# One row-tiled block per two heads in the first attention stage, with PSUM banks that change roles each cycle

## The reference

```
q = norm(x) @ Wq;  k, v = split(ctx @ Wkv)          # 16 heads of 64
p = softmax(q_h k_h^T / 8) over 12544 keys
x = x + concat_h(p v_h) @ Wo + bo
```

## Time and profile before

| what | value |
|---|---|
| median of 3 runs | 1464.38 us |
| the profiled execution's own time | 1462.08 us |
| its span, first to last instruction | 1460.4 us |
| TensorE busy | 1402.6 us, 96% |
| VectorE busy | 1067.2 us, 73% |
| ScalarE busy | 835.6 us, 57% |
| GpSimd busy | 599.9 us, 41% |
| granted TensorE clock, mean | 0.991 |

### The profile page before, as it was taken

One profiled execution on the slowest core, in us unless ns is written; L12 is line 12 of the kernel. 1 busy time (PEld: TensorE's weight loads), 2 busy tenths in 40 slices (PEclk: granted clock), 3 DMA queues, 4 the chain that ended last, 5 costly groups with the idle time before them and its releaser, 6 DMA issues. The chain is left out here.

```text
span 1460.4 us, 28153 instructions
## 1 busy us (share of the span) xinstructions
PE 1402.6 (96%) x11057; PEld 1200.8 (82%) x11057; DVE 1067.2 (73%) x2050; ACT 835.6 (57%) x1594; POOL 599.9 (41%) x521
## 2 busy tenths in 40 slices
PE   8999999999999999999999999999998889999778
PEld 7888888888888888888888888888886779999558
DVE  5777777777777777777777777777785656677774
ACT  4666666666666666666666666666662236666411
POOL 4353433435353434353535343443420427765220
PEclk9999999999999999999999999999999999999889
DMA  5000000000000000000000000000013502111720
GB/s 195 2 12 15 1 26 1 27 1 26 1 27 1 27 1 26 2 26 2 26 2 26 1 3 25 2 26 1 2 55 126 232 7 89 58 61 36 331 94 5
DMA packets 11256, 59.39 MB, mean 41 GB/s; under 512 B 2346, under 2 KB 4723, under 8 KB 10100
## 3 DMA queue, kind: packets, MB, share of 16 engines
q1 hardware_dynamic: 11124, 57.59, 10.7%
HBM read 57.45 MB, written 0.13 MB: 39 GB/s over the span
## 5 line engine op out<-in xcount | busy, mean ns | idle before, releaser
L344 POOL CAST V<-Vraw 128x512 fp32r<-128x512 f32 x189 | 115.7, 612 | 591.0 <-ACT Vraw L435 491.5
L525 DVE TENSOR_TENSOR pT<-ps,pT 128x896 fp32r<-128x896 f32 x224 | 244.4, 1091 | 140.2 <-ACT pT L427 140.0
L427 ACT ACTIVATE pT<-ps 128x896 fp32r<-128x896 f32 x224 | 205.6, 918 | 121.8 <-PE ps L606 121.0
L435 ACT COPY Vraw<-ps 128x512 f32<-128x512 f32 x189 | 111.0, 587 | 264.3 <-PE ps L586 264.3
L345 POOL TENSOR_TENSOR V<-Vraw,V 128x512 fp32r<-128x512 f32 x189 | 241.9, 1280 | 15.1
L470 DVE TENSOR_REDUCE nmx<-ps 128x1 f32<-128x896 f32 x224 | 241.9, 1080 | 0.0
L404 ACT ACTIVATE prob<-ps,nm 128x896 f32<-128x896 f32 x224 | 224.2, 1001 | 0.0
L621 PEld LDWEIGHTS ps<-pT,V 128*128 128x128 f32 x1568 | 214.9, 188 | 9.3 <-ACT d_kT L411 1.1
L621 PE MATMUL ps<-pT,V 128*128 128x256 f32 x1568 | 219.9, 279 | 0.7 <-ACT d_kT L411 0.7
L478 DVE TENSOR_REDUCE xn<-ps 128x128 f32<-128x256 f32 x224 | 95.0, 424 | 103.1 <-PE ps L621 103.1
L677 PE MATMUL ps<-ident,prob 64*128 64x64 f32 x3136 | 145.2, 229 | 4.1 <-ACT prob L404 2.6
(11 more groups left out here) (325 smaller groups left out, 2446.3 us busy)
## 6 DMA issues: line engine op xcount, KB each, us to landing
raw<-in_ctxT SPq DMA_DIRECT2D x16, 896.0 KB, 4.6
d_raw<-in_ctxT SPq DMA_DIRECT2D x12, 896.0 KB, 4.6
w<-in_w SPq DMA_DIRECT2D x2, 4096.0 KB, 19.4
wg<-in_wg SPq DMA_DIRECT2D x1, 4352.0 KB, 18.3
wu<-in_wu SPq DMA_DIRECT2D x1, 4352.0 KB, 28.1
wd<-in_wd SPq DMA_DIRECT2D x1, 4352.0 KB, 37.9
e_ea<-in_alog SPq DMA_DIRECT2D x1, 2048.0 KB, 7.2
d_mrow<-in_mask SPq DMA_DIRECT2D x14, 112.0 KB, 4.5
```

What stands on the lines that cost most here:

```text
L344: link(pool, nc.gpsimd.tensor_copy(v_high(g, i), by_head(Vraw[:, j % 2, :])), "pool_chain")
L427: nc.scalar.activation(by_row(pT[u % 2][:, :, 0, :]), pT_ps, ACT.Copy).then_inc(sem("pTh_ready"), 1)
L525: nc.vector.tensor_tensor(by_row(pT[u % 2][:, :, 1, :]), pT_ps, by_row(pT[u % 2][:, :, 0, :]).bitcast(F32), ALU.subtract).then_inc(sem("pT ...
```

## The change: what it does

Two heads, e = 2c and o = 2c + 1, now make one cycle. TensorE's order in a cycle is: transposes of e, scores of the next pair, transposes of o with four turned-back sums, and then, all with 128 rows, values, piece, weighted sum of e, values, piece, weighted sum of o. The products with 64 rows stand in one block per two heads.

Both heads' probabilities must exist at once, so there are two `prob` buffers. The banks 4 to 7 change roles from cycle to cycle: the turned probabilities of e lie in one pair of banks (4 and 5, or 6 and 7), those of o in the other; values, pieces and weighted sums go into the same banks once the turned probabilities in them are copied and split. The turned-back sums move to the tails of the score banks 0 to 3. Pieces run five steps ahead. A weighted sum now runs in its own cycle. To make space for the second `prob`, `raw` holds `aq`, `ak`, `av` and `disti` once the last context chunk is split: three loads of 256 KB and two small index patterns move from the start to the end of the stage, and SyncE waits for the loads.

The diff, cut to its core:

```diff
-    AHEAD = 4
+    AHEAD = 5
+    cycles = steps // 2
-        prob = sb("prob", [P, 2, HK], F32, keep)
+        prob = [sb(f"prob{i}", [P, 2, HK], F32, keep) for i in range(2)]
-        pT_ps = ps[:, 4:6, 0:HK].rearrange("p s (t q) -> p s t q", q=P // 2)
-        O_ps = ps[:, 4:6, HK:512]
-        OT_ps = ps[:, 6, 0:2 * P]
+        def banks(c):
+            return (4, 5) if c % 2 == 0 else (6, 7)
+        def turned_banks(u):
+            return banks(u // 2 + u % 2)
+        def value_bank(u):
+            return banks(u // 2)[0]
+        def sum_of(u):
+            bank = 5 if u == steps - 1 else banks(u // 2 + 1 - u % 2)[0]
+            return ps[:, bank, 0:2 * P]
+        def back_of(u):
+            odd = 1 if u >= steps - 2 else u % 2
+            return ps[:, 0:4, HK:512].rearrange("p (s a) n -> p a s n", a=2)[:, odd, :, :]
         def piece_bank(p):
-            return 4 + p % 4 if p < AHEAD else 7
+            return 4 + p % 4 if p < AHEAD else banks((p - AHEAD) // 2)[1]
...
# SyncE, behind the loop over chunks
+                sp.wait_ge(sem("cT_split"), 2 * (chunks + 2))
+                for name in ("aq", "ak", "av"):
+                    sp.dma_start(v[name], t[name]).then_inc(sem("band_in"), 16)
+                sp.wait_ge(sem("band_in"), 96)
...
# ScalarE
+                exp_step(1)
+                for c in range(cycles):
+                    e, o = 2 * c, 2 * c + 1
+                    act.wait_ge(sem("p_turned"), e + 1)
+                    nc.scalar.activation(by_row(pT[0][:, :, 0, :]), turned(e), ACT.Copy).then_inc(sem("pTh_ready"), 1)
+                    act.wait_ge(sem("p_turned"), o + 1)
+                    nc.scalar.activation(by_row(pT[1][:, :, 0, :]), turned(o), ACT.Copy).then_inc(sem("pTh_ready"), 1)
+                    if e in v_steps:
+                        copy_values(e)
...
+                    if e + AHEAD < steps:
+                        high_parts(e + AHEAD)
+                    if e + 2 < steps:
+                        exp_step(e + 2)
+                    if o in v_steps:
+                        copy_values(o)
...
+                    if o + 2 < steps:
+                        exp_step(o + 2)
+                    if o + AHEAD < steps:
+                        high_parts(o + AHEAD)
# VectorE
+                for c in range(cycles):
+                    e, o = 2 * c, 2 * c + 1
+                    if c >= 1:
+                        add_parts(o - 2)
+                        if o - 2 + AHEAD < steps:
+                            low_parts(o - 2 + AHEAD)
+                    dve.wait_ge(sem("pTh_ready"), e + 1)
+                    nc.vector.tensor_tensor(by_row(pT[0][:, :, 1, :]), turned(e),
+                                            by_row(pT[0][:, :, 0, :]).bitcast(F32), ALU.subtract).then_inc(sem("pTl_ready"), 1)
+                    add_denominator(e)
+                    if c >= 1:
+                        update_sums(e - 2)
+                        update_sums(o - 2)
+                    dve.wait_ge(sem("pTh_ready"), o + 1)
+                    nc.vector.tensor_tensor(by_row(pT[1][:, :, 1, :]), turned(o),
+                                            by_row(pT[1][:, :, 0, :]).bitcast(F32), ALU.subtract).then_inc(sem("pTl_ready"), 1)
+                    if e + 2 < steps:
+                        max_step(e + 2)
+                    if e + AHEAD < steps:
+                        low_parts(e + AHEAD)
+                    if o + 2 < steps:
+                        max_step(o + 2)
+                    add_denominator(o)
+                    add_parts(e)
...
# TensorE; turn(u) is the 14 transposes, for odd u with turn_sums(u - 3) and turn_sums(u - 2)
+                for c in range(cycles):
+                    e, o = 2 * c, 2 * c + 1
+                    pe.wait_ge(sem("exp_done"), e + 1)
+                    if c >= 1:
+                        pe.wait_ge(sem("o_added"), e - 1)
+                    turn(e)
+                    pe.wait_ge(sem("exp_done"), o + 1)
+                    if c + 1 < cycles:
+                        scores(c + 1)
...
+                    elif o - 2 + AHEAD < steps:
+                        pe.wait_ge(sem("kl_ready"), o - 2 + AHEAD + 1)
...
+                    turn(o)
+                    if e in v_steps:
+                        pe.wait_ge(sem("pTl_ready"), e + 1)
+                        next_values(e)
...
+                    if e + AHEAD < steps:
+                        pe.wait_ge(sem("pTl_ready"), e + 1)
+                        next_piece(e + AHEAD)
+                    pe.wait_ge(sem("pTl_ready"), o + 1)
+                    weighted_sum(e)
+                    if o in v_steps:
+                        if e in v_steps:
+                            pe.wait_ge(sem("vraw_ready"), v_steps.index(e) + 1)
+                        next_values(o)
...
+                    if o + AHEAD < steps:
+                        pe.wait_ge(sem("kl_ready"), o + AHEAD)
+                        next_piece(o + AHEAD)
+                    if o in v_steps:
+                        pe.wait_ge(sem("vraw_ready"), v_steps.index(o) + 1)
...
+                    weighted_sum(o)
```

More of the change, by code:

```diff
@@ L423, in _ @@
                         exp_step(0)
[L425 to L444, removed]
@@ L519, in _, with add_denominator @@
                 max_step(1)
-                for u in range(steps):
+                def add_denominator(u):
                     h, b = u % H0, u % 8
[L522 to L532, removed]
                     if u >= H0:
@@ L657, in _ @@
                 scores(0)
+                piece(4)
                 pe.wait_ge(sem("wv_left"), 2)
@@ L667, in _, with turn @@
                 pe.wait_ge(sem("wv_right"), 1)
[L668 to L674, removed]
+                def turn(u):
                     for k in range(NT):
-                        for s, rows in enumerate(halves):
-                            mm = nc.tensor.transpose(pT_ps[:, s, k, :],
-                                                     prob[:, :, :].rearrange("p a n -> p (a n)")[rows, k * P:(k + 1) * P],
+                        for i, rows in enumerate(halves):
+                            mm = nc.tensor.transpose(turned(u)[:, i, k, :],
+                                                     prob[u % 2][:, :, :].rearrange("p a n -> p (a n)")[rows, k * P:(k + 1) * P],
@@ L679, in _ @@
                                                      ident[rows, rows])
[L680 to L681 removed]
+                    if u >= 2 and u % 2 == 1:
+                        turn_sums(u - 3)
+                        mm = turn_sums(u - 2)
                     mm.then_inc(sem("p_turned"), 1)
[L683 to L694 removed]
@@ L716, in _, with next_values @@
-                    if u == steps - 1:
-                        pe.wait_ge(sem("consts_ready"), 1)
-                        pe.wait_ge(sem("post_in"), 32)
-                        nc.tensor.matmul(ps[:, 0, 0:D], ones[0:1, :], v["brow"][0:1, 0:D], start=True, stop=False)
-                        pe.wait_ge(sem("oT_ready"), 1)
-                        project(range(0, 4))
-                        later_keys(6, 2)
-                    if u == steps - 3:
-                        pe.wait_ge(sem("kl_ready"), steps)
-                        turn_heads((0, 1, 2, 3), 7)
+                def next_values(u):
+                    j, gn, i = v_steps.index(u), u // HG + 1, V_AT.index(u % HG)
+                    if gn % 2 == 0 and i == 0:
+                        pe.wait_ge(sem("cT_split"), gn + 2)
+                    values(gn, i, value_bank(u))
```

143 lines of the change are left out of this document (75 added, 68 removed).

## The result

The changed kernel takes 1473.03 us (median of 6 runs, 1471.32 to 1474.88) against 1464.34 for the kernel before (6 runs). The ratio is 1.0071, with a 95% interval of 1.0047 to 1.0095: 8.7 us slower, under 1%. The forecast was 1470, a change of under 1%. The profiled execution took 1474.88, its span is 1471.9.

A forecast was written before the change was run, and what follows sets the result against it. TensorE, its matmuls and the seams between them, was taken to pace the stage. Loop +6.2 us and start and end together -0.6 gave +5.6, say +6: 1470 against the median of 1464.4, range 1440 to 1490.

The forecast's parts named there:

- The visit's price: TensorE in the loop: going to the 64-row form and back costs 0.29 us; one of two per cycle is removed.
- The chain: Even head's transposes, ScalarE's copy, VectorE's split: TensorE can go on to the values 2.79 us after the transposes start.
- the stall: TensorE ahead of the even head's values: 2.45 us of own work against 2.79, so it stands still 0.34 us.
- The full cycle: TensorE's usual cycle of two heads in the loop: 9.86 us against 9.83, 80 times.
- the short one: Every fourth cycle, without the even head's values: 9.05 us against 8.91, with waits of 0.34 and 0.56, 27 times.
- The rule weighed: A change of tiling mode drains TensorE; by that alone 32 us faster. PSUM copying, which may become the limit, speaks against.
- The start: Stage start up to step 2: step 2 at 46.3 us instead of 42.60, +3.7, with TensorE idle over 3 us.
- The end: Stage end: steps 216 to 220 -1.3 us, steps 220 to 223 -3.6, behind step 223 +0.6.
- The moved loads: Three 256 KB loads moved to the stage end should land by about 1100 us, covered; bounds nothing and +5.
- The seam in the full-array block: Rival: odd values after the even weighted sum cost up to 0.19 us per cycle, 21 us, giving 1491; chance 0.14.
- The saving landed: Rival: even copy and split done by 2.45 us, each cycle gains 0.28, time 1433; chance 0.12.
- The odd exponential: Rival: ScalarE's odd-head exponential, estimated 9.7 us after the even transposes, makes scores wait; 0.4 past margin gives 1515; chance 0.08.

The follow-up runs named there:

- by_bank: Changed kernel with both turned heads copied and split bank by bank and TensorE also waiting by bank; 1426.75 us, ratio 0.9767.
- before_visit: Kernel before with one added 64x64 transpose in 64-row form between values and piece of every odd step; 1499.48 us, ratio 1.0278.
- both_halves: Changed kernel with both turned heads copied and split bank by bank, TensorE still waiting for the whole head; 1444.27 us, ratio 0.9881.
- even_halves: Changed kernel with only the even head copied and split bank by bank, the odd one whole; 1447.85 us, ratio 0.9901.
- after_tiny: Changed kernel with one small VectorE instruction between the arrival of the even head's copy and its split; 1488.82 us, ratio 1.0181.
- before_turn: Kernel before with one added 128x128 identity transpose, no change of form, between values and piece of every odd step; 1476.25 us, ratio 1.0086.
- after_again: Changed kernel, unaltered, run once more for a second profile; 1475.05 us, ratio 1.0080.

## Why the prediction was right, point by point

- **The visit's price, 0.29 per cycle.** Right, if slightly low. by_bank, the same order with nothing standing still, gains 0.34 per full cycle, and before_visit pays 0.38 with its instruction in.
- **The chain, 2.79, and the stall of 0.34.** Right: 2.78, and a bracket of 0.32. What both_halves, even_halves and after_tiny change is this chain alone. That it decides is shown from both sides: shortened by about 0.3 the cycle shrinks to 9.57, lengthened by 0.19 it grows by 0.20.
- **The full cycle, 9.86, and the short one, 9.05.** Measured 9.86 and 9.07. The two waits of the short cycle are the two forecast, with the weighted sum at 4.62 after the even transposes (4.69 forecast). The 0.07 won there was lost again: behind the wait this sum takes 0.92 and not 0.82, an extra that the forecast had left out. The second bracket is 0.34 where 0.56 was forecast. The profile counts it from the end of the piece's last row (4.28), the forecast counted from when the next block could have started (4.13); with the earlier end of the wait that is the whole difference, and the sum doesn't use the bracket. The loop's total was put at +6.2 and came to +7.4.
- **The rule weighed.** The visit's price is real, by before_visit against before_turn (some 0.25 us). That agrees with the Trainium skill, TensorEngine Tiling (Array Packing), Key Properties, by which a change of tiling mode drains TensorE. Taken alone the rule would have given 32 us less than before, 1432, which is 41 us too little. The same page's PSUM Bottleneck, by which the copying out of PSUM may become the limit, named the side that won. What limits here is the delay of one copy and one split in a row (0.92 and 1.09 us), not the load of the engines: ScalarE is busy for 58% and VectorE for 73%.
- **The start, +3.7.** Measured +4.4. Mis-sized: the pause ahead of the second scores was seen ("over 3 us", 3.38 measured), but not that the clock would fall to half behind it. The scores started at 36.79, 0.56 earlier than the forecast 37.35, and from there to step 2 it took 10.22 us where 9.0 were forecast: 2.40 and not 1.32 for the scores, 0.74 and not 0.6 for the odd transposes. TensorE's rows:

```profile
36.79 0.74 PE L649 MATMUL ps<-Kh,qh 64*128 64x448 f32 x2 [3.38 <-ACT prob L432]
37.33 0.58 PE L649 MATMUL ps<-Kl,qh 64*128 64x448 f32 x2
37.70 0.58 PE L649 MATMUL ps<-Kh,ql 64*128 64x448 f32 x2
```

A pair of scores takes 0.37 here, at a granted clock of 0.50 (1.2 GHz), and 0.20 in the loop at 1.00 (2.4 GHz); the clock comes back within the odd transposes. In after_again the same pause of 3.38 us is followed by the same fall a little later: the scores take 1.33, and the stretch of 3.52 us behind them, transposes and values, runs at 0.52.

- **The end, -1.3 - 3.6 + 0.6 = -4.3.** Measured -0.3 for steps 216 to 220, -4.0 for 220 to 223 and -0.4 behind, -4.6 together. The sum was right by terms that were off in both directions: the two cycles in the first part stayed longer than reckoned, with a wait for the later keys' copy, and the part behind step 223 was no longer than before. In after_again the end gave back 2.2 and not 4.6.
- **The moved loads, covered.** Right. GpSimd's last split ended at 1103.16, and the last load landed 3.7 us after its issue at 1104.04, 15 us ahead of the stage's end. Both are 8 us later than forecast (1095 and 1100), within the cover.
- **The rivals.** The seam in the full-array block costs nothing (0.82 and 0.46 in the rows); its price of 1491 was to lie in the range, whose edge of 1490 just misses it. The saving landed only in by_bank; both_halves and even_halves have part of it. The odd exponential doesn't decide: neither scores nor odd transposes carry a bracket in the loop. In the cycle from 501.17 its last row on ScalarE ends at 510.86, 9.7 after the even transposes, as estimated, and 0.6 ahead of the scores at 511.49:

```profile
510.66 0.20 ACT L432 ACTIVATION_READ_ACCUMULATOR prob<-ps,nm 128x1 f32 x1
```

- **The total.** The cause and the loop were forecast; that the total came within 3 us is partly luck. Start and end together were put at -0.6, and came to -0.2 in the first profile and +2.7 in the second, which is just outside the 3 either way that was stated. The span grew by 11.5 and the median by 8.7. Of the 11.5, 4.3 lie in the rest of the kernel, at a lower granted clock, and after_again did not repeat them. Why the clock falls there in one execution and not in another stays open.

## What to carry to other kernels

Putting blocks of one array form together saves a countable seam, some 0.3 us per visit here. But the block that stood between two of them was also the cover for whatever the neighbours do with its result. Before merging, count from the producer's start to the moment when its banks are free again, and compare that with the work which is left in between. If the first is longer, cut the hand-over into pieces by bank, on the copying engines and in TensorE's waits, before or together with the merge. Where two such waits follow each other, only the one that ends last is worth shortening.

## What was not expected of the hardware

A pause of TensorE of 3.38 us at the start of the stage was followed by a stretch at the lower clock, which made the six pairs of scores behind it 1.1 us longer. Two shorter pauses at the end of the kernel before were not followed by one at once; the granted clock was 1.00 from 1088.56 to 1106.29:

```profile
1091.76 0.65 PE L677 MATMUL ps<-ident,prob 64*128 64x64 f32 x14 [1.40 <-DVE U L485]
1097.20 0.65 PE L677 MATMUL ps<-ident,prob 64*128 64x64 f32 x14 [1.98 <-ACT prob L404]
```
